# A third pair of PSUM banks for the gate and up products of a quantised feed-forward stage

## What is computed

```
def fp4_quant_dequant(x):            # blocks of 16 along the last dim
    scale = max(|block|) / 6, at least 1e-12
    idx = searchsorted([.25,.75,1.25,1.75,2.5,3.5,5], |x / scale|)
    return GRID[idx] * sign(x) * scale      # GRID 0,.5,1,1.5,2,3,4,6

def fp4_linear(x, w):
    return einsum('bsk,nk->bsn', fp4_quant_dequant(x), fp4_quant_dequant(w))

xn   = layernorm(x)
gate = fp4_linear(xn, w_gate)        # 1024 -> 2816
y    = fp4_linear(xn, w_up)          # 1024 -> 2816
h    = silu(gate) * y
out  = x + attention(xn) + fp4_linear(h, w_down)   # 2816 -> 1024
```

## Time and profile before

| | us |
|---|---|
| three timed runs | 4103.53, 4198.66, 4257.51 (median 4198.66) |
| the profiled execution | 4112.47 |
| its span, slowest core | 4110.9 |
| spans of the 8 cores | 4089.2 to 4110.9 |
| VectorE busy | 2546.1 (62%) |
| TensorE matmul busy | 2520.6 (61%) |
| ScalarE busy | 1185.5 (29%) |

### The profile page before, as it was taken

One profiled execution on the slowest core, in us unless ns is written; L12 is line 12 of the kernel. 1 busy time (PEld: TensorE's weight loads), 2 busy tenths in 40 slices (PEclk: granted clock), 3 DMA queues, 4 the chain that ended last, 5 costly groups with the idle time before them and its releaser, 6 DMA issues. The chain is left out here.

```text
span 4110.9 us, 35982 instructions; the slowest of 8 cores (4089.2 to 4110.9 us)
## 1 busy us (share of the span) xinstructions
PE 2520.6 (61%) x9675; PEld 945.7 (23%) x9848; DVE 2546.1 (62%) x4009; ACT 1185.5 (29%) x1835; POOL 105.7 (3%) x199
## 2 busy tenths in 40 slices
PE   1111257218779696968879696966845644644746
PEld 1111123002222121222222121222422322222322
DVE  7888821575858677675757667513157577177575
ACT  1111112015445353545545453530012121012121
POOL 0000000000000000000000000000000000000000
PEclk9999998559979797988979797985977876877877
DMA  1111220010101010010101010023320200900202
GB/s 38 44 31 41 72 48 11 0 32 20 40 16 35 22 34 24 28 35 19 35 15 37 19 31 22 23 44 83 137 78 0 82 0 5 162 0 0 82 0 72
DMA packets 126529, 156.29 MB, mean 38 GB/s; under 512 B 77824, under 2 KB 88320, under 8 KB 124288
## 3 DMA queue, kind: packets, MB, share of 16 engines
q1 hardware_dynamic: 41056, 110.25, 8.8%
q10 hardware_dynamic: 69312, 17.31, 3.1%
q0 software_dynamic: 15968, 26.42, 2.6%
HBM read 98.89 MB, written 46.66 MB: 35 GB/s over the span
## 5 line engine op out<-in xcount | busy, mean ns | idle before, releaser
L765 ACT ACTIVATE pbuf<-psA,negB_col 128x512 bf16<-128x512 f32 x512 | 351.6, 687 | 348.9 <-PE psA L751 348.9
L765 ACT ACTIVATE pbuf<-psB,negB_col 128x512 bf16<-128x512 f32 x512 | 351.4, 686 | 286.1 <-PE psB L751 285.2
L751 PE MATMUL psA<-qT_all,kT_h 128*128 128x512 bf16 x1016 | 313.2, 390 | 3.2 <-issue 2.3
L751 PE MATMUL psB<-qT_all,kT_h 128*128 128x512 bf16 x1024 | 313.7, 388 | 0.0
L781 PE MATMUL psD<-pbuf,V_h 128*128 128x512 bf16 x976 | 294.1, 379 | 27.5 <-ACT pbuf L765 27.5
L781 PE MATMUL psC<-pbuf,V_h 128*128 128x512 bf16 x976 | 299.2, 385 | 17.9 <-ACT pbuf L765 17.8
L212 DVE TENSOR_REDUCE pbm<-wbuf 128x32 f32<-128x512 f32 (+1 forms) x136 | 91.1, 670 | 346.7 <-DMA WdqN<-wqout 139.0
L1006 PE MATMUL psE<-wgq_b,xqT_sb 128*128 128x512 bf16 (+1 forms) x371 | 101.6, 427 | 206.0 <-DVE h_t L1026 205.3
L1006 PE MATMUL psD<-wgq_b,xqT_sb 128*128 128x512 bf16 (+1 forms) x375 | 102.7, 429 | 202.0 <-DVE h_t L1026 160.6
L781 PE MATMUL psE<-pbuf,V_h 128*1 128x512 bf16 x512 | 195.3, 381 | 7.0
L781 PE MATMUL psF<-pbuf,V_h 128*1 128x512 bf16 x512 | 193.1, 377 | 7.0
(11 more groups left out here) (210 smaller groups left out, 4631.9 us busy)
## 6 DMA issues: line engine op xcount, KB each, us to landing
xbuf<-x_tok SPq DMA_DIRECT2D x16, 1024.0 KB, 6.1
rbuf<-resid_scr SPq DMA_DIRECT2D x32, 512.0 KB, 5.9
wbuf<-Wg SPq DMA_DIRECT2D x44, 256.0 KB, 2.8
wbuf<-Wu SPq DMA_DIRECT2D x44, 256.0 KB, 2.7
wbuf<-Wd SPq DMA_DIRECT2D x40, 256.0 KB, 2.7
xt_buf<-xT_own SPq DMA_DIRECT2D x8, 1024.0 KB, 6.9
resid_scr<-rstage SPq DMA_DIRECT2D x8, 1024.0 KB, 4.8
resid_scr<-obuf SPq DMA_DIRECT2D x16, 512.0 KB, 4.7
```

The costliest lines, as they stand in the source:

```text
L751: ins = (lambda e, h=h, qq=qq, kc=kc, m=m, pb=pb: e.matmul(pb[:, :], kT_h[:, m, kc * 128:(kc + 1) * 128], qT_all[:, 2 * h + m, qq * 512:(q ...
L765: eb.em('scalar', lambda e, cglob=cglob, pb=pb: e.activation(out=pbuf[:, cglob % 2, :], in_=pb[:, :], func=AF.Exp, bias=negB_col[:], scale ...
```

## The change

A third pair of banks, psC0 and psC1, joins the two pairs of the gate and up products, and the pairs are taken by `s_ % 3`. TensorE waits for the product three chunks back and no longer for the one two chunks back. Since the down product uses psC0 and psC1 as well, TensorE waits at the start of each half until every eviction of the down product before it is done. In the first half there is none before it and no wait.

```diff
         for half in range(2):
             toff = half * 1024
             eb.wait('scalar', S['avq'], S['avq'].n)
+            eb.wait('tensor', S['ffdn'], S['ffdn'].n)
             for tt in range(8):
                 eb.wait('vector', S['aab'], S['aab'].n)
                 for ci, (c0, clen) in enumerate(NCH):
                     s_ = half * 24 + tt * 3 + ci
-                    pg, py = [(psD0, psD1), (psE, psF)][s_ % 2]
-                    if s_ >= 2:
-                        eb.wait('tensor', S['hbld'], hb_base + s_ - 1)
+                    pg, py = [(psD0, psD1), (psE, psF), (psC0, psC1)][s_ % 3]
+                    if s_ >= 3:
+                        eb.wait('tensor', S['hbld'], hb_base + s_ - 2)
```

## The result

The changed kernel takes 4006.76 us (median of 8 runs, 4003.46 to 4014.05) against 4107.15 us (median of 6 runs, 4103.53 to 4152.61): the ratio is 0.9759, with a 95% interval from 0.9746 to 0.9771. That is 100 us, or 2.4%, less. The experiments were timed in other series, in which the kernel before had medians from 4110.31 to 4129.57 us, so a ratio compares better than a time in us. The profiled execution took 4007.24 us, 105.2 us less than that of the kernel before. Its lines are numbered one higher from L998 on: L1006 is L1007 here, L1022 is L1023, L1026 is L1027.

What follows compares the result with a forecast made beforehand. VectorE was taken to bound the feed-forward tiles, idling while chunk 2 waited for a PSUM pair. 115.1 - 9.8 - 2.3 = 103.0 us off 4112.47 gave 4009.5 us, range 3988 to 4165.

Steps and rivals of the forecast that it cites:

- The gap and its count: Before the 384-wide product of chunk 2: VectorE's gap falls from 4.69 to 0.67 us, 30 gaps, gain 115.1 us.
- the two paced tiles: First tile of each weight group's second half, where TensorE sets the pace; its 1.81 us gap was not counted.
- The transposes: The third group of transposes, slower after TensorE's rest, delays Abs and L228: 0.35 us in 28 tiles, 9.8 us cost.
- the second rival: ScalarE's chain replaces the gap: Abs another 0.6 us later a tile, 17 us lost, time 4026; chance 0.08.
- The added wait: At a half's start TensorE waits for the down product's last eviction: 1.16 us late, counted twice, 2.3 us cost.
- TensorE's cover: In each tile, TensorE has the next chunk 2 ready between 14.7 and 23.7 us; it is needed at 25.66.
- The first rival: TensorE's clock stays low through all tiles; 28 tiles each lose up to 0.64 us more, time 4027; chance 0.10.
- The third, no effect: An overlooked wait in TensorE's queue keeps chunk 2 from being early; time 4115; chance 0.05.
- The fourth: The clock stays low in the down products too, 4.6 instead of 2.37 us each; time 4170; chance 0.03.
- the hand-over between the weight groups: Between the two weight groups: length unchanged, since the second group's weight loads and the tile-7 copies move together.
- the likeliest case: The forecast itself over the tiles, with transposes costing 0 to 16 us: time 4000 to 4016; chance 0.74.
- the slower rival: Low clock in 64 groups of down matmuls, paced by TensorE alone: 143 us lost, time 4170; chance 0.03.

Runs made afterwards that it cites:

- the same gs_c buffer: Two buffers for gs_c instead of one: on the changed kernel ratio 0.9638, median 3966.25 us; on the kernel before, with two pairs of banks, ratio 0.9988.

## Why the prediction was right

**The gap and its count held.** I forecast 0.67 us in place of 4.69 and found 0.69. The tile took 23.45 us for the 23.42 of the prediction. Over the 30 places the idle time before the 384-wide product fell from 135.2 to 21.3 us, 113.9 where I had 115.1; the two paced tiles kept their 1.81. The old wait put back brings the gap and the thirty waits back, so the cause is shown. The first tiles of the weight groups, which I counted for ScalarE's late queue, did gain (0.69 us in both).

**The transposes held to the hundredth.** VectorE's wait for Abs grew from 11.4 to 21.2 us in 28 times, 9.8 us. That was the number forecast from the one rested group of the earlier trace rows, 0.35 us a tile. Two runs show its two halves. With Abs ahead of the copies it vanishes, so it comes through ScalarE's queue. With TensorE kept busy it is there in the tiles in which the third group is slow and not in the others. So the second rival, a later Abs by another 0.6 us a tile, is out too.

**The added wait was a little dearer.** 1.28 us for 1.16, in two places as said: TensorE starts 0.26 us after an eviction's end, not 0.14 as after a product. It is 0.2 us in all.

**TensorE's cover held.** I had chunk 2 ready 14.7 to 23.7 us into the tile; for the tile above it was ready 17 us into the tile before (TensorE rests from 3094.35 on, 6.84 us, before its transposes start at 3101.19, and the tile before began at 3077.4), 8.8 us before its Silu began at 3103.11. 9.5 us more of matmuls in each tile left most tiles at 23.08 to 23.45 us. The first rival, TensorE at the low level and VectorE waiting for it, is out with that. The third, no effect, went with the 30 waits. The fourth is out as well: in the first down product the clock was 0.99 where the earlier trace rows have 1.00, both from 3.6 us after its first matmul on, as these stretches of the changed kernel show.

```profile
core 7: us, PE busy (x) PEld busy (x) DVE busy (x) ACT busy (x) POOL busy (x), PEclk, DMA share, GB/s
3000.00:3170.00 170.00, 99.22 (x419) 50.34 (x417) 140.50 (x119) 39.64 (x54) 0.00 (x0) 0.75 0.05 10
3202.18:3236.18 34.00, 34.00 (x156) 15.25 (x155) 9.63 (x14) 0.00 (x0) 0.00 (x0) 0.99 0.54 189
```

Over the tiles it is 0.75, the value of the earlier trace rows, while VectorE is busy 140.50 of 170 us, 83% where it was 72%. TensorE's rests ahead of chunk 2 are gone and those ahead of the transposes have come. The Trainium skill, TensorE: Matmul & The Clock Gate, "A second HAM failure mode: psum-queue depth-cycling", would have had throughput fall. The clock does swing here, but it did so before, and what the change adds to its cost is the 0.35 us a tile above, where VectorE waits for Abs behind the slow transposes.

**The sum.** 113.9 less 9.8 less 2.6 is 101.5 us; the medians differ by 100.4. The profiled executions differ by 105.2. Of that, 1.8 lie ahead of the stage's first product (3007.34 and not 3009.10), and the hand-over between the weight groups, less one tile, is 3.8 us shorter and the shortest of all the traces; I had it unchanged. The stretches with the other down products took about 1.5 us more than the late start explains. So the hit of the forecast time within 3 us is partly luck; that of the terms is not.

**The time.** I gave 4009.5 on the profiled execution's own time and a range up to 4165 for the spread of the runs shown. Four of the five further runs of the kernel before lay within 6 us of its fastest and one 49 us above it, so the upper part of the range was not needed; the median fell into the 4000 to 4016 that I gave for the likeliest case alone.

**Two slips that changed nothing.** The chances add up to 0.83 for faster by over 2% and 0.14 for within 2%, not 0.82 and 0.15. And the price of the slower rival took all four down products as paced by TensorE alone: in the one at the end of the first weight group it already stood still for 15.3 us in the kernel before (14.6 after), waiting for VectorE's evictions.

## What to carry to other kernels

Where a fixed number of chunks is made per tile and the consumer then goes away for long, the ring of PSUM banks should hold the whole tile's chunks: with one pair too few, one chunk in each tile starts only when the consumer comes back, and its full length shows. The Trainium skill says as much of buffers in general (Perfetto Trace Analysis, "Identifying Performance Opportunities": the same gap repeating can mean that PSUM ran out), and the 30 nearly equal gaps here agree. Then look again for the wait that ends last: the same gs_c buffer was worth nothing before the third pair and 40 us after it. And where an engine takes its list in order, put what the limiting engine waits for ahead of what nobody waits for soon.

## What I had not expected of the hardware

Three 128x128 transposes of f32 took 0.52 us in one tile and 0.87 us in the next, with the granted clock at 1.00 and at 0.50, although TensorE had been idle for the same 2.68 us before both and its two groups ahead of that rest had run alike (0.60 us each). So the length of the rest just before does not decide alone; what does is open. Making the rest ahead of the first group shorter, from 6.8 us to 4.0, changed nothing. The hand-over between the weight groups lasts as long as ScalarE's queue takes to issue 27 DMA transposes, and that differs by up to 5.6 us between traces of kernels that do the same there; why is open.
